# Cross attention and expert layers on one core: GpSimd's weight splitting held back behind VectorE's normalization, and a reordered start and last step

## What is computed

```python
x = x + _L0_xattn_ref(_layernorm(x, axis=-1), ctx_4096, L0_xattn_Wq, L0_xattn_bq, ...)   # 32 heads of 128, 8 key/value heads
x = x + _L0_ffn_ref(_layernorm(x, axis=-1), L0_ffn_gate_w, L0_ffn_up_w, ...)
x = x + _L1_xattn_ref(_layernorm(x, axis=-1), ctx_4096, L1_xattn_wq, ...)                # 32 heads of 16
x = x + _L1_ffn_ref(_layernorm(x, axis=-1), L1_ffn_W_gate, L1_ffn_b_gate, ...)           # 8 experts, all computed, 2 averaged
```

## Time and profile before

| what | value |
|---|---|
| median of 3 runs | 1761.13 us (1760.33 to 1764.64) |
| the profiled execution, its own time | 1759.08 us |
| its span | 1757.3 us |
| TensorE busy | 1684.8 us, 96% of the span |
| VectorE busy | 1200.8 us, 68% |
| ScalarE busy | 709.4 us, 40% |
| GpSimd busy | 524.6 us, 30% |
| mean granted clock of TensorE | 0.989 of full |

### The profile page before, as it was taken

One profiled execution on the slowest core, in us unless ns is written; L12 is line 12 of the kernel. 1 busy time (PEld: TensorE's weight loads), 2 busy tenths in 40 slices (PEclk: granted clock), 3 DMA queues, 4 the chain that ended last, 5 costly groups with the idle time before them and its releaser, 6 DMA issues. The chain is left out here.

```text
span 1757.3 us, 31909 instructions
## 1 busy us (share of the span) xinstructions
PE 1684.8 (96%) x12480; PEld 887.0 (50%) x12480; DVE 1200.8 (68%) x2269; ACT 709.4 (40%) x1290; POOL 524.6 (30%) x401
## 2 busy tenths in 40 slices
PE   5879999999999999999999999998999999999998
PEld 2445555555555555555555444444444545455443
DVE  6786666665656656656566667777878888888873
ACT  5543333333333333333333433233544555545442
POOL 4143560701605307117500110010023333332334
PEclk9899999999999999999999999999999999999999
DMA  7031150411512404215421130112544544545440
GB/s 270 13 92 42 49 180 13 144 49 25 168 25 62 131 14 127 66 25 181 133 74 25 45 118 1 25 25 52 194 98 80 93 76 91 91 83 92 74 83 19
DMA packets 235373, 142.57 MB, mean 81 GB/s; under 512 B 219232, under 2 KB 219488, under 8 KB 227296
## 3 DMA queue, kind: packets, MB, share of 16 engines
q1 hardware_dynamic: 167648, 123.82, 26.3%
q10 hardware_dynamic: 67584, 16.79, 5.4%
HBM read 65.60 MB, written 20.97 MB: 49 GB/s over the span
## 5 line engine op out<-in xcount | busy, mean ns | idle before, releaser
L813 PE MATMUL bank<-R 128*128 128x512 f16 (+1 forms) x7152 | 1295.6, 341 | 28.7 <-DVE X L1800 11.6
L813 PEld LDWEIGHTS bank<-R 128*128 128x128 f16 x7152 | 585.1, 98 | 678.0 <-issue 34.9
L1712 DVE SCALAR_TENSOR_TENSOR R<-bank,biases,R 128x512 f16<-128x512 f32 x288 | 204.6, 746 | 221.1 <-ACT R L1295 178.2
L668 POOL TENSOR_TENSOR R<-R 128x512 f32<-128x512 f32 x112 | 144.8, 1293 | 321.9 <-ACT R L1504 319.6
L1295 ACT ACTIVATE R<-bank,biases 128x512 f16<-128x512 f32 x128 | 87.7, 686 | 271.6 <-PE bank L813 267.3
L524 POOL TENSOR_SCALAR R<-R 128x2048 f32<-128x2048 f32 (+1 forms) x21 | 34.8, 1656 | 385.4 <-PE bank L813 351.8
L1504 ACT ACTIVATE R<-R,msk 128x512 f32<-128x512 f32 x128 | 90.1, 718 | 118.2 <-DVE R L2081 118.1
L1800 DVE SCALAR_TENSOR_TENSOR X<-bank,X 128x512 f32<-128x512 f32 x128 | 86.7, 683 | 33.5 <-PE bank L813 33.4
L1724 DVE SCALAR_TENSOR_TENSOR R<-bank,R 64x512 f16<-64x512 f32 x64 | 44.0, 688 | 94.7 <-ACT R L1303 94.2
L2081 DVE SCALAR_TENSOR_TENSOR R<-bank,R 128x512 f32<-128x512 f32 x128 | 85.4, 679 | 29.5 <-PE bank L813 28.8
L1303 ACT ACTIVATE R<-bank 64x512 f16<-64x512 f32 x128 | 75.6, 591 | 50.7 <-PE bank L813 49.6
(11 more groups left out here) (161 smaller groups left out, 1630.4 us busy)
## 6 DMA issues: line engine op xcount, KB each, us to landing
R<-in_wB SPq DMA_DIRECT2D x16, 1024.0 KB, 5.1
R<-in_wX SPq DMA_DIRECT2D x16, 1024.0 KB, 4.8
w_split<-AW SPq DMA_DIRECT2D x16, 1024.0 KB, 4.8
R<-w_split SPq DMA_DIRECT2D x12, 1024.0 KB, 7.4
R<-in_ctxT SPq DMA_DIRECT2D x4, 1024.0 KB, 9.9
X<-in_x SPq DMA_DIRECT2D x4, 1024.0 KB, 13.7
out<-X SPq DMA_DIRECT2D x16, 256.0 KB, 2.0
R<-in_wB SPq DMA_DIRECT2D x7, 512.0 KB, 5.6
```

The lines of the kernel that those rows point to most:

```text
L668: g.tensor_tensor(acc, acc, tmp[:, e % 2, :], ALU.add).then_inc(e_acc, 1)
L813: last = pe.matmul(dst, a(sa), b(sb_), start=(k == 0), stop=(k == m - 1))
L1712: v.scalar_tensor_tensor(out=dst, in0=src, scalar=bias, in1=hi, op0=ALU.add, op1=ALU.subtract).then_inc(done, 1)
```

## The change

GpSimd gets four waits. `ctx_rest(1)` waits until the lo halves of chunks 0 and 1 are done (`n_lo` of 8). Piece 6 waits for the two lo halves of step 0's probabilities (`s_plo` of 2). Piece 8 waits until the lo halves of chunk 3 are done (`n_lo` of 16, in step 1), and piece 9 for the probabilities of step 2 (`s_plo` of 6).

In steps 0 and 1 VectorE's `add` of tile 0 moves ahead of the context's lo half, and that of tile 1 ahead of `xnorm(2)`. TensorE issues all four `b_out` with one pair of transposes behind the first and one at the end, and waits for the stored tiles behind the scores of the following step. ScalarE stores transposed tile 1 ahead of `hi(2)`. In the last step each half of the probabilities is sent off before the other is finished, the four `b_pv` stand together, and norm and output work follow them in a new order. Before step 0, VectorE's `proj_lo(0, 0, 1, 3)` moves in among the statistics of chunk 1. VectorE's loop over steps 4 to 27 is written out.

```diff
@@ gpsimd
+            pool.wait_ge(n_lo, 2 * TC)
             ctx_rest(1)
             pool.wait_ge(ctx_lo, 2)
             pool.wait_ge(o0_in, 16)
+            pool.wait_ge(s_plo, 2)
             split(6, raw_o0, *halves(R2, 6144, 2048))
...
             group_piece(7, 0, 2, 1, 1, raw_kv1)
+            pool.wait_ge(n_lo, 4 * TC)
             group_piece(8, 1, 2, 1, 0)
+            pool.wait_ge(s_plo, 6)
             group_piece(9, 1, 3, 1, 2)
@@ tensor, b_step
+                if isinstance(s, int) and 0 < s <= 2:
+                    pe.wait_ge(n_stored, (s + 2) * TC)
...
-                    b_pv(s, 0)
-                    b_pv(s, 1)
+                    for jb in range(4):
+                        b_pv(s, jb)
+                    b_out(s, par, 0)
                     turn(0)
                     turn(1)
-                    b_pv(s, 2)
-                    b_pv(s, 3)
-                    b_out(s, par, 0)
                     b_out(s, par, 1)
+                    b_out(s, par, 2)
                     turn(2)
                     turn(3)
-                    b_out(s, par, 2)
                     b_out(s, par, 3)
...
                 if early:
-                    for t in range(TC):
+                    b_out(s, par, 0)
+                    turn(0)
+                    turn(1)
+                    for t in range(1, TC):
                         b_out(s, par, t)
-                        if t % 2 == 0:
-                            turn(t)
-                            turn(t + 1)
-                    pe.wait_ge(n_stored, norm + TC)
+                    turn(2)
+                    turn(3)
@@ scalar, b_step, last step and early steps
                     phi(0)
+                    turn(0)
                     phi(1)
-                    turn(0)
                     turn(1)
+                    for jb in range(4):
+                        o_part(s, g, jb)
                     hi(0)
                     hi(1)
-                    o_part(s, g, 0)
-                    o_part(s, g, 1)
                     turned_x(0)
+                    hi(2)
                     turned_x(1)
-                    o_part(s, g, 2)
-                    o_part(s, g, 3)
-                    hi(2)
                     hi(3)
...
                 turned_x(0)
+                turned_x(1)
                 hi(2)
-                turned_x(1)
@@ vector, last step
+                    plo(0)
                     prob(1)
-                    plo(0)
                     plo(1)
                     add(s - 1, c - 1, 2)
                     add(s - 1, c - 1, 3)
+                    olo(0)
+                    olo(1)
                     chunk_newton(dve, norm // TC)
                     dve.wait_ge(st_out, 16 * NX)
                     xnorm(0)
                     xnorm(1)
+                    olo(2)
+                    olo(3)
                     xlo(0)
                     xlo(1)
-                    olo(0)
-                    olo(1)
+                    add(s, c, 0)
                     xnorm(2)
+                    xlo(2)
                     xnorm(3)
-                    olo(2)
-                    olo(3)
-                    add(s, c, 0)
-                    xlo(2)
                     xlo(3)
@@ vector, steps 0 and 1
                     xlo(0)
                     xlo(1)
                     if early:
+                        add(s, c, 0)
                         dve.wait_ge(ctx_hi, s + 3)
...
                 if early:
+                    add(s, c, 1)
                     xnorm(2)
-                    add(s, c, 0)
+                    xnorm(3)
                     xlo(2)
-                    add(s, c, 1)
-                    xnorm(3)
                     xlo(3)
@@ vector, ahead of step 0, and the loop
-            chunk_stats(dve, 1, lambda t: x_tile(TC + t))
-            proj_lo(0, 0, 1, 3)
+            for t in range(TC):
+                if t == 3:
+                    proj_lo(0, 0, 1, 3)
+                v.bn_stats(cbn[:, t, :], x_tile(TC + t)).then_inc(n_bn, 1)
+            chunk_var(dve, 1)
...
-            with dve.Fori(0, 3) as i:
-                for k in range(8):
-                    b_step(i * 8 + (NC + k), k % NC, i * 2 + (1 + k // NC), i * 2 + (1 + (k + 1) // NC), False,
-                           first_again=k == 0)
-            for s in range(28, 32):
-                b_step(s, s % NC, s // NC, (s + 1) // NC, s == 31, NT if s == 31 else None)
+            for s in range(NC, NG * NC):
+                b_step(s, s % NC, s // NC, (s + 1) // NC, s == NG * NC - 1, NT if s == NG * NC - 1 else None)
```

More of the change, by code:

```diff
@@ L1726, in proj_lo, with b_step @@
                     last.then_inc(p_lo, 1)
-            def b_step(s, c, g, gn, last, norm=None, first_again=False):
+            def b_step(s, c, g, gn, last, norm=None):
                 first = None if norm is None else norm % NT
@@ L1796, in add @@
                     dve.wait_ge(y_mm, s * 4 + t + 1)
-                    if t == 0 and not isinstance(s, int) and not first_again:
+                    if t == 0 and NC <= s < 2 * NC:
                         dve.wait_ge(bo_added, (c + 1) * TC)
```

## The result

The changed kernel takes 1744.91 us (median of 4 runs, 1743.83 to 1745.77), the kernel before beside it 1761.86 us: a ratio of 0.9906, 95% interval 0.9892 to 0.9921. It is faster by 17 us where 26 were forecast, and 1745 lies above the range of 1730 to 1741 us. The profiled execution's span fell from 1757.3 to 1741.8 us, its own time from 1759.08 to 1743.83 us.

What follows compares the result with a forecast made beforehand. TensorE was busy for 96% of the span, so only its waits and slow running could be won. Gains of 22.3 + 3.2 + 0.4 = 25.9 us gave 1733.2, or 1735 us as median; range 1730 to 1741 us.

Steps and rivals of the forecast that it cites:

- Ahead of step 0: Before step 0's projections: VectorE's norm chain runs without GpSimd beside it, so they start 6.2 us sooner.
- rival 3: Ahead of step 0 and in the last step the clock stays up: 2 to 3 us more gained, 1732 us; chance 0.13.
- Piece 6: GpSimd's piece 6 in step 0: hidden by 2 us, its shadow on a small statistics operation costing 0.3 us.
- Ends of steps 0 and 1, step 2: Fewer waits and slow matmuls: 6.3 us at step 0's end, 9.9 at step 1's, 0.7 in step 2.
- The new chain on GpSimd.: Piece 8, its buffer's next load, piece 9: ready at 130.3 us, so TensorE waits 0.5 us in step 3.
- Rival 1: GpSimd becomes the bound in step 3, with piece 8 or 9 ending 3 us later: 1738 us; chance 0.12.
- The loop: VectorE's steps 4 to 27 written out: pauses before steps 12 and 20 go, TensorE gets 3.2 us back.
- rival 2: VectorE's pause is not the loop's, so unrolling gives at most 0.2 us: 1738 us; chance 0.09.
- Last step: New order in the last step: output work 1.0 us sooner, partly lost to the clock; gain 0.4 us.
- Rival 4: Only the orders help; VectorE is slow ahead of step 0 for another reason: 1743.5 us; chance 0.05.

Runs made afterwards that it cites:

- x6: The changed kernel without its four waits on GpSimd: 1753.5 us, ratio 0.9964 to the kernel before.
- x7: The kernel before with the four waits on GpSimd alone: 1749.0 us, ratio 0.9937 to the kernel before.

## Why the prediction was right or wrong

The mechanisms were right in direction; the time was not, because one cost was left out and one was too small. Between the two profiled executions 15.3 us were won of 25.9: the start lost 4.7 us against the forecast (item 4), the last step 1.8 (item 6), and the parts that nobody edits 3.7 (item 7).

1. *Ahead of step 0*, 6.2 us forecast: 6.3 us up to step 0's `b_pv` (62.04 to 55.72). The refinement took 0.79 us, xn and lo their undisturbed durations. Right in the mechanism, and `x6` and `x7` show that GpSimd was the cause. That the number fits so well is partly luck: the projections start only 5.1 us sooner, and the other 1.2 us is clock (10.8 us for them instead of 12.1), which the forecast had left to rival 3; the repeat of the same kernel was 2.0 us later. One row was also read for more than it is: the operation of 1.87 us (L692) has one SBUF input, not two.
2. *Piece 6* was hidden as forecast (done at 60.45, needed at 62.74 us), and the shadow on the small operation was 0.08 us (0.25 instead of 0.17) instead of 0.3.
3. *Ends of steps 0 and 1, step 2*: 22.8 us forecast at step 2's third projection, 22.6 measured: 5.7 us between the first `b_pv` of steps 0 and 1 (6.0 forecast) and 10.5 from there on (10.6). How much of it belongs to the waits was only learned in `x6`.
4. *The failed step: "The new chain on GpSimd."* I followed what piece 8's new place releases, and found the load and piece 9. I took the load's 5.27 us as GpSimd's time alone and did not ask what else moves data while it runs. Its place moved from 25 us ahead of step 2's transposes to 0.6 us ahead of them, and the second load, released by the same count, stood behind it. Two loads in front of the transposes cost TensorE 3.9 us of waiting and 1.7 us of clock; taking them away gives 5.3 us in stretch A, 4.7 us in the medians on one chip. That is over half of the missing 9 us. Rival 1, which had GpSimd's chain late for TensorE, named the wrong victim: piece 9 was in time, and the wait of 0.5 us that the sum had for it was none.
5. *The loop*, 3.2 us forecast: 3.1 us from step 11 to step 30. These pauses of 1.6 to 2 us went with the loop. The Trainium skill's price of about 108 ns for a compare-and-branch ("Advanced Engine Details and Errata", Control Flow Timing), by which rival 2 was weighed, does not cover them.
6. *Last step*, +0.4 us forecast with bounds -0.7 and +1.2: -1.4 us in the profile. The gain of the order was 0.5 to 1.0 us where the clock stayed up; the term mis-sized is the clock's, up to 2.2 us instead of up to 1.7, and it came in six of eight profiles where I had taken about half of its 1.7 us. TensorE's first wait was also not the transposes but an addition (1.58 us): with half 0's lo part moved ahead, VectorE finishes half 1's probabilities later, stands 0.70 us for ScalarE's hi half (at 964.30 us), and the two additions come behind that.
7. *The rest*, 0 forecast: in the profiles 3.7 us were lost between the feed-forward part and the end (19.2 us ahead at the last gate of the feed-forward part, 15.5 at the end). 1.65 us of it is the clock's fall around 1211 us, and 2 us lie in layer 2. Repeats of one kernel differ by up to 1.3 us in the first and 1.4 us in the second, so part of it can be chance; whether the rest is tied to the change (the fall came in every profile with the new last step, layer 2 took longer in eight of the nine with the written-out loop than in any with the loop) stays open.

The chances were right on the sign. Rival 4 (only the orders help) had nearly the measured time, 1743.5 us, but its mechanism is refuted by `x6` and `x7`: a number that fits does not show the cause. The range was too narrow at its upper end because it was built from rivals that each moved one term, and had none for data transfers that meet.

## What to carry to other kernels

A wait that delays an engine also delays everything its counter releases, and each released transfer lands in a new place: list the transfers and look at what else is in flight in that place, above all short ones that TensorE needs at once. Where large loads would go out just ahead of short transposes that TensorE waits for, let the large ones be released by the short ones' landing; here that gave 4.7 us more on one chip and 7 us by the ratios from two, and the kernel with both loads late (1737.5 and 1739.6 us) is the fastest of all. Putting GpSimd's work where VectorE's operations don't meet it was worth more than the stalls that the trace names, in part because matmuls behind such stalls ran at the lower clock (twelve took 5.28 and 4.18 us instead of 2.76).

## What the runs showed of the hardware

- A pair of DMA transposes held its queue for 2.65 us with no load in flight, 4.89 us behind one load of 1 MB and 7.28 us behind two. The loads themselves were hardly slower for it (piece 9's arrived after 5.17 us, 5.27 before).
- An operation of VectorE on 128x4 elements took 0.16 us alone and up to 1.87 us beside GpSimd; an operation with one input in PSUM and one in SBUF (L1715) took 0.75 us at 54.69 us, beside GpSimd's piece 6, as elsewhere. The Trainium skill says the same ("SBUF — State Buffer", Who interferes with whom): with at most one SBUF input, and outside its two-port modes, a VectorE operation does not meet GpSimd; with two it does. One SBUF input alone was no protection here: the xn operations (L736, of the form TENSOR_SCALAR, with one SBUF tensor) took 2.58 us for two beside GpSimd and 1.00 us without it.
- The clock fell at different places though the instructions around were the same: 12 matmuls of the last step took 2.76 to 4.93 us in kernels with one order of it, 24 matmuls behind the feed-forward part 5.34 us in three profiles and 6.3 us or more in ten.
